# Keeping q on chip in token blocks, with adjacent load columns in the maximum pass and maxima turned on TensorE

## The reference, cut to what matters

```
xn = layernorm(x)                       # 8 batches, 256 tokens, 512
q, k, v = split(xn @ Wqkv)              # q: 32 heads of 16; k and v: one head of 16
s = q . k / 4 + slope[head] * (pos_k - pos_q), masked where pos_k > pos_q
attn = softmax(s) @ v ; x = x + attn @ Wo + lora_mixture(xn)
x = x + attention2(layernorm(x)) + silu(gate) * up @ down     # second layer
```

## Time and profile before

| what | value |
|---|---|
| runs | median 640.08 us of 3 (638.49 to 640.99) |
| profiled execution | 638.76 us, span 636.9 us |
| TensorE busy | 587.7 us, 92% of the span, granted clock 0.958 of full on the mean |
| VectorE busy | 479.8 us, 75% |
| ScalarE busy | 373.4 us, 59% |
| GpSimd busy | 352.3 us, 55% |

### The profile page before, as it was taken

How to read it: one execution, slowest core, us unless ns; L and a number is a source line. 1 busy time by engine, 2 the same in 40 slices (tenths; PEclk the granted TensorE clock), 3 DMA queues, 4 the chain that set the end, 5 groups by cost and what they waited for, 6 DMA issues and landing times.

```text
span 636.9 us, 14221 instructions
## 1 busy us (share of the span) xinstructions
PE 587.7 (92%) x5582; PEld 437.5 (69%) x5582; DVE 479.8 (75%) x1050; ACT 373.4 (59%) x695; POOL 352.3 (55%) x363
## 2 busy tenths in 40 slices
PE   5767956699999999999999999999999999999997
PEld 3746623566886688756877587867885877785783
DVE  4687999799989599968789649994787468654642
ACT  3343769747755586555848475756564886652240
POOL 4332779434646487546548654765575776652230
PEclk9977985799999999999999999999999999999999
DMA  9869698601310143012500150005100100000000
GB/s 243 107 133 186 165 216 194 79 2 38 52 18 5 67 104 33 4 33 68 69 3 3 43 94 2 3 15 97 10 3 22 48 1 1 34 3 1 34 1 33
DMA packets 38290, 36.11 MB, mean 57 GB/s; under 512 B 8912, under 2 KB 28272, under 8 KB 38224
## 3 DMA queue, kind: packets, MB, share of 16 engines
q1 hardware_dynamic: 29488, 24.41, 18.9%
q0 software_dynamic: 2720, 8.49, 6.5%
q10 hardware_dynamic: 6016, 2.31, 1.5%
HBM read 30.28 MB, written 8.39 MB: 61 GB/s over the span
## 4 chain that ended last, share of the span: by engine, by line
PE 65%; DVE 21%; issue 5%; DMA 3%; ACT 3%; POOL 2%; SPq 1%; ACTq 0%; DVEq 0%
PE B_bank L1236 24%; PE B_bank L1257 15%; PE A_bank L1188 6%; PE B_bank L1129 4%; PE A_bank L1161 4%; DVE mx L1510 4%; PE A_bank L1095 3%; PE E_bank L1145 3%; PE E_bank L1141 1%; DVE probs L1526 1%; DVE hf L1626 1%; DVE st L1377 1%; DMA q_parts<-qs 1%; DVE nmp L1519 1%; PE B_bank L1224 1%
## 5 line engine op out<-in xcount | busy, mean ns | idle before, releaser
L857 POOL TENSOR_TENSOR probs<-e,probs 128x512 f16<-128x512 f32 x176 | 209.9, 1198 | 151.6 <-ACT probs L980 150.8
L1236 PE MATMUL B_bank<-xs,wgu 128*128 128x256 f16 x1792 | 206.8, 273 | 0.0
L979 ACT ACTIVATE e<-E_bank,wn 128x512 f32<-128x512 f32 x192 | 133.1, 693 | 121.1 <-PE E_bank L1145 56.6
L1236 PEld LDWEIGHTS B_bank<-xs,wgu 128*128 128x128 f16 x1792 | 174.0, 98 | 23.3 <-DVE hf L1616 0.5
L980 ACT ACTIVATE probs<-E_bank,wn 128x512 f16<-128x512 f32 x192 | 133.3, 694 | 0.0
L1257 PE MATMUL B_bank<-wd,hbuf 128*128 128x512 f16 x448 | 100.0, 379 | 1.1 <-DVE hf L1626 1.1
L1510 DVE TENSOR_REDUCE mx<-B_bank 128x8 f32<-128x256 f32 (+6 forms) x168 | 88.0, 579 | 4.9 <-PE B_bank L1129 4.5
L871 POOL TENSOR_TENSOR hbuf<-hf,hbuf 128x512 f16<-128x512 f32 x56 | 66.1, 1181 | 38.9 <-ACT hbuf L1008 38.7
L1257 PEld LDWEIGHTS B_bank<-wd,hbuf 128*128 128x128 f16 x448 | 43.5, 98 | 50.4 <-DVE hf L1626 1.4
L1616 DVE SCALAR_TENSOR_TENSOR hf<-ebuf,B_bank 128x512 f32<-128x512 f32 x56 | 38.2, 683 | 44.4 <-ACT ebuf L1018 44.2
L1129 PE MATMUL B_bank<-kk,qq 128*128 128x32 f16 (+20 forms) x512 | 64.3, 269 | 4.6 <-issue 2.4
(11 more groups left out here) (198 smaller groups left out, 690.7 us busy)
## 6 DMA issues: line engine op xcount, KB each, us to landing
qq<-q_parts SPq DMA_DIRECT2D x21, 256.0 KB
x<-in_x SPq DMA_DIRECT2D x20, 256.0 KB, 3.6
out_y<-x SPq DMA_DIRECT2D x16, 256.0 KB, 2.0
xa<-in_x SPq DMA_DIRECT2D x12, 256.0 KB, 4.7
q_parts<-qs SPq DMA_DIRECT2D x12, 256.0 KB, 2.6
wgu<-in_gate_w POOLq DMA_DIRECT2D x4, 448.0 KB, 7.8
wgu<-in_up_w POOLq DMA_DIRECT2D x4, 448.0 KB, 6.9
wd<-in_down_w POOLq DMA_DIRECT2D x4, 448.0 KB, 6.7
```

The lines of the kernel that those rows point to most:

```text
L857: pool.tensor_tensor(probs[:, u % PSLOTS, 1, :], e32[:, w, :], probs[:, u % PSLOTS, 0, :], ALU.subtract).then_inc(s_lop, 1)
L979: act.activation(e32[:, w, :], psum("exp", i, g, w)[:, :], ACT.Exp, scale=wn[:, 7:8])
L1236: mm = pe.matmul(psum(name, u, i)[:, a * SEQ:(a + 1) * SEQ].rearrange("p (t n) -> p t n", t=NU), wgu[:, m, k, (2 * i + a) * P:(2 * i + a + ...
```

## The change

1. `qq` is laid out as [row, batch, block of 32 tokens, head, token of the block]; tokens are no longer permuted. A load of the maximum pass is 128 adjacent columns: 4 heads x 32 tokens of one block. All loads of a block see the same keys (32 to 256 of them). There are again 64 loads and 21 groups a batch.
2. `q_parts` in DRAM is laid out by part, batch, block, tile, dimension, head and token, so that a gather reads and writes runs of 8 heads x 32 tokens. A store writes runs of one block of one row. Each q tile is stored by four transfers (two batches x two parts).
3. The rows of a q tile on partitions become (dimension, head) in place of (head, dimension): for chunk 0 by a copy of Wq with turned columns (`turn`, on POOL), later in `hi`.
4. Chunk 0's q tiles have a slot each (`q_first`, in the space of the feed-forward's down weights), so nothing waits for a slot.
5. The maxima [128, 64] are turned by TensorE (`nmT`), ScalarE makes the high part and VectorE the low part from PSUM as [64, 128], and SP writes 64 runs of 256 bytes for each part.
6. Token rows of both batches are made by VectorE (eight copies); the 1 MB transfer goes. The slope and position rows go to `qq` by four transfers in place of six.
7. Wo and LoRA's B are loaded from SP's queue right after the constants, not from POOL's queue later.
8. `pv` on VectorE writes the reciprocal into PSUM in place and frees the bank after the product, not after the reciprocal. `attnT` is copied straight.
9. The planner gets other costs for the changed steps and new constants in `RANK` (all of them), with a fourth one for batch 0 or chunk 1. So the order of steps changes on every engine.

```diff
-TR = 4
-NJ = SEQ // TR
-JT = P // TR
+GH = 4
+GT = P // GH
+NTB = SEQ // GT
+NHB = NH // GH
+NG = NTB * NHB
...
+    out = []
+    for tb in range(NTB):
+        width = GT * (tb + 1)
+        steps = -(-NHB // min(NHB, 512 // width))
+        for n in range(steps):
+            h0, h1 = NHB * n // steps, NHB * (n + 1) // steps
+            out.append((tb, h0, h1 - h0))
...
-        p.add("DVE", ("max", i, n), pe("max", i, n), *([dve("nm", i - 2)] if i > 1 else []))
-    p.add("DVE", ("nm", i), dve("max", i, NMG - 1))
-    p.add("SP", ("nm", i), dve("nm", i))
+        p.add("DVE", ("max", i, n), pe("max", i, n), *([pe("nmT", i - 2)] if i > 1 else []))
+    p.add("PE", ("nmT", i), dve("max", i, NMG - 1))
+    p.add("ACT", ("nmT", i), pe("nmT", i), *([sp("nm", i - 1)] if i else []))
+    p.add("DVE", ("nmT", i), act("nmT", i))
+    p.add("SP", ("nm", i), dve("nmT", i))
...
+        p.add("SP", ("wo",), sp("consts", gap=0.0))
...
-        p.add("PE", ("q0", b, m), act("xT0", 0, 2 * b), act("xT0", 0, 2 * b + 1), at=9.0 + m)
-        p.add("ACT", ("q0", b, m), pe("q0", b, m), dve("scale"), *([("ACT", ("store", b, m - 2), 2.5)] if m > 1 else []))
+        p.add("PE", ("q0", b, m), act("xT0", 0, 2 * b), act("xT0", 0, 2 * b + 1), pool("turn", m))
+        p.add("ACT", ("q0", b, m), pe("q0", b, m), dve("scale"))
...
+        q_first = wd[:, 0:NB * NK, :].rearrange("p (b m) (a t) -> p b m a t", b=NB, a=2)
...
-        qq = sb("qq", [P, NB, NH, SEQ], F16)
-        mx = sb("mx", [P, NB, NJ], F32)
-        nmp = sb("nmp", [P, NB, 2, NJ], F16)
+        qq = sb("qq", [P, NB, NTB, NH, GT], F16)
+        mx = sb("mx", [P, NB, NG], F32)
+        nmp = sb("nmp", [NG, 2, P], F16)
...
-        q_dram = nc.dram_tensor("q_parts", [2, NH * HD, 2, NB, SEQ], F16).ap()
+        q_dram = nc.dram_tensor("q_parts", [2, 2, NB, NTB, NK, HD, P // HD, GT], F16).ap()
...
+        def store_heads(eng, c, b, m, source, stored):
+
+            for part in range(2):
+                eng.dma_start(q_dram[c % 2, part, b, :, m, :, :, :].rearrange("c d h t -> (d h) c t"),
+                              source[:, part, :].rearrange("p (c t) -> p c t", t=GT)).then_inc(stored, 16)
...
+                rows = qq[HD * g:HD * g + HD, b, :, h0:h1, :]
+                if len(tiles) == 1:
+                    eng.dma_start(rows.rearrange("d c h t -> d c (h t)"),
+                                  q_dram[c % 2, part, b, :, tiles[0], :, :, :].rearrange("c d h t -> d c (h t)")).then_inc(s_gather[b], 16)
+                else:
+                    eng.dma_start(rows.rearrange("d c (m h) t -> d (c m) (h t)", m=NK),
+                                  q_dram[c % 2, part, b, :, :, :, :, :].rearrange("c m d h t -> d (c m) (h t)")).then_inc(s_gather[b], 16)
...
+                for dst, source in ((wo_sb[:, 0:NK, :], wo.rearrange(kp, p=P)), (wo_sb[0:NE * LR, NK, :], lora_b),
+                                    (wo_sb[NE * LR:P, NK, :], lora_b)):
+                    sp.dma_start(dst, source).then_inc(s_wo, 16)
...
-                sp.dma_start(q_dram[c % 2, m * P:(m + 1) * P, :, :, :],
-                             qs[:, m % 2, :, :].rearrange("p a (b t) -> p a b t", b=NB)).then_inc(s_qd[m], 16)
-
-            def hot_rows():
-                sp.wait_ge(s_hotrow, 1)
-                sp.dma_start(qq[R_HOT:P, 1, :, :], hot.unsqueeze(1).broadcast_to([P - R_HOT, NH, SEQ])).then_inc(s_hot[1], 16)
+                for b in range(NB):
+                    store_heads(sp, c, b, m, qs[:, m % 2, :, b * SEQ:(b + 1) * SEQ], s_qd[m])
...
+                                 .rearrange("o (g n) -> o g n", n=P), nmp[:, part, :]).then_inc(s_nmrow[b], 16)
...
+            def turn(m):
+                cols = slice(m * P, (m + 1) * P)
+                pool.wait_ge(s_wq[m], 16)
+                pool.tensor_copy(wq_turned[:, :, cols].rearrange("p k (d h) -> p k d h", d=HD),
+                                 wq_sb[:, :, cols].rearrange("p k (h d) -> p k d h", d=HD)).then_inc(s_turned, 1)
...
-                if m >= 2:
-                    act.wait_ge(s_q0[b][m - 2], 16)
...
+                if n - 2 >= NK:
+                    act.wait_ge(s_qd[(n - 2) % NK], 16 * 2 * NB * ((n - 2) // NK))
+                act.activation(qs[:, m % 2, 0, :], psum("q", c, m)[:, :], ACT.Identity, scale=SCALE / (XS * WS)).then_inc(s_qh, 1)
...
+            def nmT(i):
+                wait_full(act, "nmT", i)
+                if i:
+                    act.wait_ge(s_nmrow[(i - 1) % 2], 32 * ((i - 1) // 2 + 1))
+                act.activation(nmp[:, 0, :], psum("nmT", i)[0:NG, 0:P], ACT.Copy, scale=-1.0 / NM).then_inc(s_nmh, 1)
...
-                    mm = pe.matmul(acc[:, g, :], qq[:, b, :, :].rearrange("p h (r j) -> p (h r) j", r=TR)[:, :, j],
-                                   keys.rearrange("p t k -> p (t k)")[:, 0:width], start=True, stop=True, skip_group_check=True)
+                    tokens = qq[:, b, tb, GH * (h0 + g):GH * (h0 + g + 1), :].rearrange("p h t -> p (h t)")
+                    mm = pe.matmul(acc[:, g, :], tokens, keys.rearrange("p t k -> p (t k)")[:, 0:width], start=True, stop=True,
+                                   skip_group_check=True)
...
+                pe.transpose(psum("nmT", i)[0:NG, 0:P], mx[:, i % 2, :], identf[:, :]).then_inc(full("nmT", i), 1)
...
+                acc = psum("exp", i, g, w)[:, :].rearrange("p (h c t) -> p c h t", h=HG, t=GT)
+                tokens = qq[:, b, :, HG * g:HG * g + HG, :]
                 if w == 1:
-                    mm = pe.matmul(acc[:, :, :], kk[:, b, 0, 1, :], tokens[:, :, JT:2 * JT], start=True, stop=True)
+                    mm = pe.matmul(acc[:, :, :, :], kk[:, b, 0, 1, :], tokens[:, NTB // 2:NTB, :, :], start=True, stop=True)
...
+                blocks = R_HOT // GT
+                c0 = blocks * (n % 4)
+                dve.tensor_copy(qq[R_HOT:P, n // 4, c0:c0 + blocks, :, :],
+                                hot.rearrange("p (c t) -> p c t", t=GT).unsqueeze(2).broadcast_to([P - R_HOT, blocks, NH, GT]))\
+                   .then_inc(s_hot[n // 4], 1)
...
-                mv = mx[:, b, :]
-                link(dve.tensor_scalar(nmp[:, b, 0, :], mv, -1.0 / NM, None, ALU.mult))
-                dve.scalar_tensor_tensor(out=nmp[:, b, 1, :], in0=mv, scalar=-1.0 / NM, in1=nmp[:, b, 0, :],
-                                         op0=ALU.mult, op1=ALU.subtract).then_inc(s_nmp, 1)
+            def nmT(i):
+                dve.wait_ge(s_nmh, i + 1)
+                dve.scalar_tensor_tensor(out=nmp[:, 1, :], in0=psum("nmT", i)[0:NG, 0:P], scalar=-1.0 / NM, in1=nmp[:, 0, :],
+                                         op0=ALU.mult, op1=ALU.subtract).then_inc(free("nmT", i), 1)
...
+                link(dve.reciprocal(pvb[:, :, 2 * HD], pvb[:, :, 2 * HD]))
```

More of the change, by code:

```diff
@@ new lines @@
+    "POOL": {"start": (338, 0.5, 34, 23), "ffn_load": (-280, 1, 13, 3), "ln0": (468.5, 1, -41, 144), "clear": (-81.5, 2, -1, -103),
+        "turn": (176, 4, -29, 20), "norm": (-170, 1, -10, 39), "late": (244.5, 4, 0, 29), "norm2": (-191, 3, -46, 131),
+        "lo": (520, -2, -13, -11), "setup1": (-258.5, 1, -53), "setup2": (491.5, 3, -40, 154), "exp": (-533, 4),
+        "ln1": (-398, -2, -24, -97), "att4": (416, -2, -81, 153), "up": (-667.5, 0.5, -49, -52)},
+    "SP": {"x_load": (361, 4, 3, 2), "consts": (395, -2, -26, 1), "wo": (438, 2, 247, -23), "gather_first": (-18, 3, -6, -235),
+        "gather": (68, 2, -86, -160), "tables": (142, 1, -7, 41), "q": (952.5, 4, -60, 97), "nm": (211, 1, 0, 264),
+        "x1_load": (-206.5, 2, -14), "down": (215.5, 2, 0, 129)},
@@ L148, in cost @@
     if engine == "PE" and step[0] == "max":
-        j0, count = MAXG[step[2]]
-        return 0.02 + count * max(0.114, TR * (j0 + count) / 2400 + 0.02)
+        tb, _, count = MAXG[step[2]]
+        return 0.02 + count * max(0.05, GT * (tb + 1) / 2400 + 0.01)
+    if engine == "DVE" and step[0] == "max":
+        tb, _, count = MAXG[step[2]]
+        return 0.08 + count * GT * (tb + 1) / 1000
     if engine == "PE" and step[0] in ("qa", "q", "tok") and step[1]:
@@ L158, in rank @@
 def rank(engine, step):
-    base, by_chunk, first = (RANK[engine][step[0]] + (0,))[0:3]
+    base, by_chunk, first, own = (RANK[engine][step[0]] + (0, 0))[0:4]
     if step[0] not in BY_BATCH and step[0] not in BY_CHUNK:
@@ L163, in rank @@
     c = step[1] // 2 if step[0] in BY_BATCH else step[1]
-    return base + by_chunk * c + (0 if c else first)
+    return base + by_chunk * c + (0 if c else first) + (own if step[1] == (0 if step[0] in BY_BATCH else 1) else 0)
 class Plan:
@@ L333, in query @@
         p.add("PE", ("q", c, m), pe("qa", c, m, gap=0.0))
-        c2, m2 = (n - 2) // NK, (n - 2) % NK
-        old = [("ACT", ("store", b, m2), 2.5) for b in range(NB)] if c2 == 0 else [sp("q", c2, m2)]
-        p.add("ACT", ("q", c, m), pe("q", c, m), *old)
+        p.add("ACT", ("q", c, m), pe("q", c, m), *([sp("q", (n - 2) // NK, (n - 2) % NK)] if n - 2 >= NK else []))
         p.add("DVE", ("q", c, m), act("q", c, m))
```

(12 more changed lines are left out.)

235 lines of the change are left out of this document (99 added, 136 removed), and 21 rows, old and new, of tables (RANK, US).

## The result

The changed kernel takes 625.06 us (median of 4 runs, 625.01 to 626.89), the kernel before 640.0 us beside it. The ratio is 0.9773, with a 95% interval of 0.9746 to 0.9799: 15 us less. The profiled execution has a span of 623.2 us, against 636.9.

The account below looks back on a forecast made before the run. TensorE's work was taken to bind from 160 to 480 us, order and waits before. Terms - 14 - 2 - 7 + 1 + 1 + 0.5 + 1 + 1 = - 18.5 gave 620.3, set at 621; range 605 to 646.

Parts of the forecast that it names:

- The term of - 27 us: Maximum pass on TensorE: adjacent columns make loads 97 instead of 197 ns, so 37.2 us of work replace 64.3.
- The 73 ns of a pair: Maximum pass: assumed TensorE time of one load and matmul with adjacent columns, read from line 1224, against 126 ns before.
- Three quarters of 19 us: Six later batches' maximum passes: share of TensorE's saved work expected to shorten the run, 14 us.
- The reduces: VectorE in the maximum pass: 9216 columns a batch instead of 8724, costing 4.1 us more, near 92 us busy.
- The split: Splitting the maxima: transpose, ScalarE copy and one VectorE step replace two slow steps, giving VectorE back 12 us (9 to 14).
- the reciprocals in place: Attention sums: in-place reciprocals hold a bank one VectorE step longer, costing 0.5 us.
- 7 + 2 us of gains: Start: 7 us from removed waits (q slots 1, wo load 3, line 1519 3), 2 us from passes of batches 0 and 1.
- 3 of costs: Start: 1 us each for batch 1's token rows on VectorE, the tail of a store, and ScalarE's extra store issues.
- the term of + 1 us: Start: ScalarE issues 16 first stores instead of 8, 4 to 11 us falling where it waited for slots; 1 us added.
- The price of a store: q stores in 64-byte runs: 25 ns a packet taken, 6.4 us a tile, so nothing waits but a store's tail.
- rival B: Stores are dear, delaying the first maximum of batches 0 and 2: at 62 ns a packet 663 us; chance 0.17.
- Signs that were to mean a wrong prediction: Stores above 12 us, TensorE waiting for a gather, or VectorE ending most gaps from 180 us on.

## Why the prediction came out as it did

621 was forecast and 625.1 measured, faster as forecast and in the range. That it came so near is in part luck: terms were wrong in opposite directions.

- **The load.** Right in kind: 100 ns where 97 were foreseen. The term of - 27 us was mis-sized, it measured 64.3 - 47.7 = 16.6. The 73 ns of a pair were read from groups of 16 matmuls, and a group's busy time holds its last matmul to the end. Groups of line 1154 have 2 to 8, and a group of 4 costs 100 ns a pair. And the old pairs were not all bound by their loads: with the step again in the changed kernel, 64 pairs take 6.6 us in place of 2.9 at 32 columns, but 9.3 in place of 9.0 at 192.
- **How much is captured.** Three quarters of 19 us, 14, were foreseen of the six later batches. Of 12.7 us of TensorE's work, 10.1 came in the changed kernel; in the kernel before 1.8 of 10.6, and 4.3 of 10.0 beside the faster multiplication. The fraction was about right, and that VectorE must have room for it fits the waits of line 1129. What gave the room is open: the multiplication gave a part, and the prediction's answer, the order of the steps, was not tried by itself.
- **VectorE.** The reduces were to rise to about 92 us: 92.1. The split was to take under 0.4 us and give back 12: line 1543 takes 0.25 to 0.28, and 12.3 us came.
- **The step that failed: the reciprocals in place, costed at + 0.5 us.** Only the longer hold of the bank was priced, and not the operand that the multiplication reads. It is worth 6.7 us in the kernel before and 8.2 in the changed one, more than the waits at the start gave and not far from the 10.1 of the loads. The row that said so (585 ns for 128 elements, between lines with four times as many at 680) was in the profile and was not read.
- **The start.** 7 + 2 us of gains against 3 of costs (the token rows, the tail of a store, ScalarE's stores) were foreseen, but TensorE's idle time before 160 us rose by 6 us. ScalarE no longer waits 3.35 us for a slot at 31.4 us, but it stands 5.77 us behind its own stores in the same place; this was the term of + 1 us that counted on cover from the old wait, and the run with long runs gives it 5.1. Of the waits of the earlier trace rows, that for xa is 0.8 us and that for lora_b gone. That for qs is not: with line 1519 gone, TensorE stands 4.18 us at 70.8 us for a q step that now comes behind seven small steps of the LoRA mixture in VectorE's order.
- **The price of a store.** 25 ns a packet, bounds of 22 to 69. A further 64-byte packet costs 5 to 9 ns of a DMA engine, below the lower bound. By engine time rival B was wrong by far. Its places, ahead of the first passes of batches 0 and 2, were about right. What the term lacked is the issue: two stores held ScalarE for 5.6 us, and four behind six large loads held SP for 23.7.
- **The signs.** Signs that were to mean a wrong prediction did appear. Three stores took 21 to 26 us to land, above the 12, though the median was 3.0. TensorE stood waiting, not for a gather but for what stood behind the stores. And VectorE ends 1.5 of the 1.7 us of waits that the profile names from 180 us on, which is too little to matter. The time was still near, because 8 us of VectorE's multiplication, unforeseen, made up for the start.

Added up by undoing, in the changed kernel: loads 10.1, reciprocals 8.2, short runs - 6.5, together 11.8 of 15.0 us. The 3 us left fall to the split of the maxima, the waits and the order of the first steps, which were not tried one by one; that the parts add up is itself not shown. Open also is why the issue of 64-byte stores stalls, behind large loads or, at 26 us, without them; the runs show when it does, and that longer runs do not there.
